# Expert numbers packed five to a word and loaded once into TensorE's registers

## What is computed

```
gates = softmax(xt @ Wg.T)                  # 16 experts
scores, inds = top_k(gates, 2)              # two experts for each token
scores = scores / sum(scores)
h = silu(xt @ We_gate[e].T) * (xt @ We_up[e].T)
y_sel = h @ We_down[e].T                    # for the two experts e of the token
y = sum(y_sel * scores) + sigmoid(xt @ Wsg.T) * shared_expert(xt)
```

## Time and profile before

| | us |
|---|---|
| median of 3 runs without the profiler | 518.58 |
| lowest and highest of them | 518.02, 519.61 |
| span of the profiled execution | 535.7 |
| TensorE busy in it | 516.2 (96%) |
| VectorE busy | 401.4 (75%) |
| ScalarE busy | 277.7 (52%) |
| GpSimd busy | 173.2 (32%) |

### The profile page before, as it was taken

One profiled execution on the slowest core, in us unless ns is written; L12 is line 12 of the kernel. 1 busy time (PEld: TensorE's weight loads), 2 busy tenths in 40 slices (PEclk: granted clock), 3 DMA queues, 4 the chain that ended last, 5 costly groups with the idle time before them and its releaser, 6 DMA issues.

```text
span 535.7 us, 10052 instructions
## 1 busy us (share of the span) xinstructions
PE 516.2 (96%) x3475; PEld 470.2 (88%) x3475; DVE 401.4 (75%) x842; ACT 277.7 (52%) x466; POOL 173.2 (32%) x161
## 2 busy tenths in 40 slices
PE   8999999999999699998999999999999999999997
PEld 6898898898888689988889989898989898989897
DVE  6997466898985466666666458998796969697986
ACT  4696865246652354444444545654453627272751
POOL 0001121101027565566662170517060424224302
PEclk9999999999999899999999999999999999999999
DMA  8926275122025355774456550443034111212112
GB/s 308 411 111 256 90 284 216 32 59 60 31 79 165 121 159 158 226 246 159 162 157 146 167 179 12 113 163 89 20 111 166 59 60 50 61 39 81 39 40 80
DMA packets 29840, 69.16 MB, mean 129 GB/s; under 512 B 4992, under 2 KB 9472, under 8 KB 28768
## 3 DMA queue, kind: packets, MB, share of 16 engines
q1 hardware_dynamic: 22496, 49.68, 25.8%
q0 software_dynamic: 6864, 18.75, 13.1%
q10 hardware_dynamic: 432, 0.09, 0.1%
HBM read 41.24 MB, written 27.26 MB: 128 GB/s over the span
## 4 chain that ended last, share of the span: by engine, by line
PE 81%; DVE 8%; issue 3%; another core or an unknown queue 3%; ACT 2%; DMA 1%; POOL 0%; SPq 0%; POOLq 0%; DVEq 0%; ACTq 0%
PE ps L771 52%; PE ps L981 9%; PE ps L777 6%; PE ps L911 6%; PE ps L1013 4%; PE ps L866 1%; ACT blk_xT L1105 1%; DVE blk_xT L1311 1%; PE ps L928 1%; DVE pT L1311 1%; DMA rows_y<-ytab,slot 1%; DVE probs_f L1646 1%; PE ps L875 1%; DVE place_hot L1497 1%
## 5 line engine op out<-in xcount | busy, mean ns | idle before, releaser
L758 POOL DMA_INDIRECT rows_y<-ytab,slot x64 | 77.6, 1213 | 148.1 <-DVE acc L1661 131.7
L738 POOL DMA_INDIRECT blk_x<-rows,row x79 | 81.0, 1025 | 79.4 <-DVE row L1512 30.5
L771 PE MATMUL ps<-vv,pT 128*128 128x258 f32 x768 | 97.6, 284 | 0.0
L771 PEld LDWEIGHTS ps<-vv,pT 128*128 128x128 f32 x768 | 95.2, 189 | 1.0
L771 PE MATMUL ps<-xT,shared_w 128*128 128x512 f32 x384 | 92.7, 394 | 0.4 <-DVE sil L1389 0.3
L771 PEld LDWEIGHTS ps<-xT,shared_w 128*128 128x128 f32 x384 | 70.7, 188 | 15.5 <-issue 0.9
L771 PE MATMUL ps<-qT,xbT_hi 128*128 128x512 f32 x256 | 79.3, 391 | 0.0
L981 PE MATMUL ps<-expert_w,blk_xT 128*128 x474 | 66.9, 290 | 5.8 <-DVE blk_xT L1311 5.3
L981 PEld LDWEIGHTS ps<-expert_w,blk_xT 128*128 128x128 f32 x474 | 59.5, 191 | 8.4 <-issue 8.3
L771 PEld LDWEIGHTS ps<-qT,xbT_hi 128*128 128x128 f32 x256 | 47.0, 188 | 9.2
L1299 ACT ACTIVATE probs_f<-probs_f 128x1024 f32<-128x1024 f32 x32 | 33.5, 1048 | 35.4 <-DVE probs_f L1646 35.4
(11 more groups left out here) (166 smaller groups left out, 857.7 us busy)
## 6 DMA issues: line engine op xcount, KB each, us to landing
ytab<-blk_y SPq DMA_DIRECT2D x40, 256.0 KB
keys<-xT SPq DMA_DIRECT2D x8, 1024.0 KB, 6.1
stage_e<-in_experts SPq DMA_DIRECT2D x16, 384.0 KB, 3.1
rows<-xn SPq DMA_DIRECT2D x8, 512.0 KB, 3.5
xbT_hi<-keys SPq DMA_DIRECT2D x8, 512.0 KB
xbT_lo<-keys SPq DMA_DIRECT2D x8, 512.0 KB
out<-acc SPq DMA_DIRECT2D x32, 128.0 KB
acc<-in_x SPq DMA_DIRECT2D x7, 512.0 KB, 9.0
```

Of the source, the lines that this page charges most:

```text
L738: e.indirect_dma_start(out=blk_x[:, q, n, :], out_offset=None, in_=rows, in_offset=bass.IndirectOffsetOnAxis(ap=row[:, 2 * b + n:2 * b + n ...
L758: e.indirect_dma_start(out=rows_y[:, r, k, :], out_offset=None, in_=ytab, in_offset=bass.IndirectOffsetOnAxis(ap=slot[:, k, i:i + 1], axis=0),
L771: ins = e.matmul(dst, stationary(p, k), moving(q, k), start=(n == 0), stop=(n == total - 1))
```

## The change

Expert numbers are below 16, so they fit in 4 bits (`BITS`). VectorE first clamps the 80 numbers in float (`blk_m`), and then packs five (`PACK`) into one by Horner's rule, sofar * 16 + next, four times, on 16 numbers at once. The last of the four writes integers to `blk_e`, now 16 words. TensorE loads all 16 words with one TENSOR_LOAD at the place of the first one of before; the other 19 are gone. `expert_of[n]` becomes an expression, shift right and mask, which is worked out in the registers at each block's gate and up products, once for a block (the lowest of five needs no shift). The down products go on from a register that the gate and up products left. The count that TensorE waits for in `routed` grows from 21 to 25.

```diff
+BITS = 4
+PACK = 5
...
         if 0 < b < PAIRS:
-            if b % 2 == 0:
-                steps.append(("blk_ids", b))
             steps.append(("blk_gate_up", b))
...
-        ROUTED = {"ek": 2, "gap": 3, "hot": 6, "totals": 7, "summed": 14, "slots": 18, "blocks": 21}
+        ROUTED = {"ek": 2, "gap": 3, "hot": 6, "totals": 7, "summed": 14, "slots": 18, "blocks": 20 + PACK}
...
-                    _, values = nc.values_load_multi_w_load_instructions(
-                        blk_e[0:1, 2 * b:2 * b + 4], engines=[mybir.EngineType.PE], min_val=0, max_val=NE - 1,
+                    _, packed = nc.values_load_multi_w_load_instructions(
+                        blk_e[0:1, :], engines=[mybir.EngineType.PE], min_val=0, max_val=(1 << BITS * PACK) - 1,
...
-                    for n, value in enumerate(values):
-                        expert_of[2 * b + n] = value
+                    for n in range(USED):
+                        expert_of[n] = (packed[n // PACK] >> (BITS * (n % PACK))) & (NE - 1)
...
-                        e.tensor_scalar(blk_e[:, :], blk_f[:, :], float(NE - 1), None, ALU.min).then_inc(routed, 1)
+                        e.tensor_scalar(blk_m[:, :, :], blk_f[:, :].rearrange("p (r j) -> p r j", j=PACK), float(NE - 1),
+                                        None, ALU.min).then_inc(routed, 1)
+                        for j in range(PACK - 2, -1, -1):
+                            e.wait_ge(routed, at + PACK + 1 - j)
+                            sofar = blk_m[:, :, PACK - 1] if j == PACK - 2 else blk_s[:, j + 1, :]
+                            e.scalar_tensor_tensor(out=blk_e[:, :] if j == 0 else blk_s[:, j, :], in0=sofar,
+                                                   scalar=float(1 << BITS), in1=blk_m[:, :, j], op0=ALU.mult,
+                                                   op1=ALU.add).then_inc(routed, 1)
```

More of the change, by code:

```diff
@@ L488, in build @@
         blk_f = own("blk_f", [P, BLOCKS])
-        blk_e = own("blk_e", [P, BLOCKS], I32)
+        blk_m = own("blk_m", [P, BLOCKS // PACK, PACK])
+        blk_s = own("blk_s", [P, PACK, BLOCKS // PACK])
+        blk_e = own("blk_e", [P, BLOCKS // PACK], I32)
         bqk = own("bqk", [P, 2, KD])
```

## The result

The changed kernel takes 518.93 us (median of 20 runs, 518.26 to 520.10), the kernel before 518.0 us (20 runs beside them, 517.2 to 519.61). The ratio is 1.0016, with a 95% interval from 1.001 to 1.0022: slower by 0.5 to 1.1 us. That lies within the 0.3% that were called no change, but on the other side of the forecast of 518.2: 0.4 us less was forecast, 0.9 us more came. (The prediction had 518.58 us for the kernel before, the median of three runs; twenty give 518.0.)

What follows compares the result with a forecast made beforehand. TensorE was taken to bound the kernel. 518.58 - 1.0 (late completions) + 0.6 (longer load) + 0 (register instructions) + 0 (VectorE) = 518.2 us, range 515.5 to 520.3.

Steps and rivals of the forecast that it cites:

- the first term: Among the blocks: TensorE's completions told late behind loads would go with the nineteen loads, -1.0 us.
- the load of pair 24 holds completions back: Late blocks: waits behind this load read as completions told late, 0.94 us lost in two pairs.
- the 17 us between span and median: Profiled execution of the kernel before, 17.1 us over its median: most waits among the blocks taken as absent without the profiler.
- The 3 us: Stretch of the blocks: about 20 us not TensorE's work less 17.1, the most late completions could cost in the median.
- The sign that I named against it: Last load, at 293.1 us with gathers over: ScalarE waits only 0.28 us, so loads may not delay completions.
- The long load: The one remaining load, ahead of the first blocks, brings 16 words instead of four: a stall of +0.6 us.
- Rival D: Long load alone at the first load's price per word, no gain: 520.0 us, by the skill's page 521.1; chance 0.06.
- The register instructions: On TensorE's sequencer at each block: 142 added, about 0.1 us each, hidden by its lead, 0 us.
- Rival C: Sequencer bounds each pair's gate and up start, bare register instructions behind the wait: 520.6 us for eight pairs; chance 0.06.
- VectorE: Packing ahead of the blocks: four chained instructions, 0.84 us, absorbed by idle time, 0 us.
- The profiled span: Profiled execution after the change: near 528 us if loads hold completions back, 536 if not.

Runs made afterwards that it cites:

- e5: The changed kernel itself beside the kernel before, on a chip where the kernel before takes about 538.5 us: 538.62 us, ratio 1.0005.
- e9: Kernel before with block tokens brought from fixed rows by SyncE's plain transfers instead of GpSimd's gathers: 527.86 us, kernel before beside it 540.19.
- e1: Changed kernel with the sixteen packed words loaded a second time right behind the first load, odd blocks using the second copy: 538.58 us, ratio 1.0002.
- e15: Changed kernel with the sixteen words loaded twice, fixed rows by SyncE and the first keys' transfers issued by ScalarE: 527.6 us.
- e18: Changed kernel with its load behind the last wide products, fixed rows by SyncE, keys' transfers spread over pairs 13, 18, 23 and 28: 524.72 us.
- e17: Kernel before with fixed rows by SyncE and the first keys' four transfers issued by ScalarE at pairs 13, 18, 23 and 28: 524.69 us.
- e4: Kernel before, all twenty loads kept, with 158 register instructions added (numbers times 16, shift and mask per block): 541.19 us, ratio 1.0044.
- e7: Kernel before with 158 register instructions added and all loads kept, run again on a second chip: 541.72 us, ratio 1.0057.
- e12: Kernel before with 158 register instructions added, all loads kept, and fixed rows by SyncE instead of gathers: 531.97 us.
- e14: Changed kernel with fixed rows by SyncE and the first keys' transfers issued by ScalarE: 525.75 us.
- e16: Changed kernel with its load behind the last wide products, fixed rows by SyncE and the first keys' transfers issued by ScalarE: 526.15 us.

## Why the prediction was wrong, and where it was right

**The step that failed is the first term**, -1.0 us for late completions behind the loads. It came from two readings. One was that the load of pair 24 holds completions back, by the earlier trace rows. e5 has such waits, the same rhythm of two pairs and the same span without a load among the blocks; e9 has all the loads and none of the waits. What the runs show in place of the -1.0 is 0. The other was that the 17 us between span and median are the profiler's. They go with the chip: the runs of the kernel before gave 538.5 us there. This reading happened to keep the term small, since it left 3 us to gain; but it was a wrong reason, and that was luck. The 3 us weren't there either. They came from taking all forty pairs at 2.80 us, and in the changed kernel's trace three pairs take 3.52, 3.52 and 3.70 because products of other steps stand in them, 2.3 us of work. The sign that I named against it, no wait behind the last load, was the right one to follow: at 293.1 us there is still a load, and the gathers are over.

**The long load**, +0.6 us, was right in mechanism and about right in size: 1297 ns for 16 words, 81 ns a word against my 83, so 1.30 us against 1.33, and 0.72 us of stall. The price was per word, near enough; a second load of sixteen right behind the first took 1.12 us in e1 and 1.11 in e15. The Trainium skill ("Runtime: NRT & Kernel Launch", section "Instruction fetch mechanics") gives about 200 ns a register, by which I had estimated 3.2 us for the sixteen; for this load from SBUF the trace disagrees, with 1.30. Rival D, which had this end, fell.

**The register instructions**, 0, were right in the steady pace: pairs stay at 2.80 us, and e18 against e17 shows no loss. One is 36 ns long and holds the sequencer for about 0.1 us (two cost 0.19), as I had taken it. But the term is not quite 0: I had priced the two that stand bare wherever TensorE waits for VectorE's copy at 0.1 to 0.25 us, and left them out because few such waits would be left. One is left at pair 2 in the changed kernel's trace, and the two cost 0.19 us there. Rival C had the right mechanism for another kernel: where the loads stay, as in e4, e7 and e12, the instructions come with 2.6 to 4.1 us. It did not come about because the change takes the loads away at the same time.

**VectorE**, 0: right as far as the trace shows; the four operations took about 0.85 us, 147.84 to 148.69, as worked out, and the last `row_f` sum wasn't later than the execution as a whole.

**The sum** with the first term at 0, the load at 0.72 and one bare pair of register instructions at 0.19 is 518.0 + 0.9 = 518.9, against 518.93 measured. The two places are read from traces; that they are the loss is supported and not proved by a run on its own: doubling the load costs more (e15 over e14, 1.9 us, a part of it the clock), and with the load covered no loss is seen (e18, to within 0.8 us). One rival stands: the wait of 1.25 us at 227.00 us, for a store, if it is in most runs of the changed kernel and in few of the kernel before. The changed kernel with the load moved was never timed with its gathers on a chip of the 518 kind; on those of the 538 kind it made no difference. A version that beats both kernels wasn't found: with everything hidden the change can only come back to the time before.

**The profiled span**, 528 or 536, was neither: 518.0, a span of the other kind of chip, where the changed kernel's runs have 516.3 to 518.1.

## What to carry to other kernels

Compare two profiles only after their spans have been held against medians of the same chip; here a span 17 us over its own median meant that the trace was of other conditions, not that the profiler took a toll. Before a wait is put down to an instruction that stands next to it in time, look for a place where the one occurs without the other, as in the earlier trace rows. A step on TensorE's sequencer was free here up to the array's queued work, so one long step cost what many short ones didn't: look where the widest products stand and put it behind them. In the traces that closed the gap; that it saves the time was not measured. And count all that stands in one lead: loads and register instructions were each hidden alone, and not together.

## What the runs showed of the hardware

- The same kernel took 518.0 and 518.37 us on two occasions and 538.5 to 540.2 us on four others, each of these on another chip. On the slow ones the engines wait among the gathers for completions that the rows can't attribute, and late in the blocks the array loses 0.5 us a pair (3.27 to 3.33 against 2.80). With plain transfers instead of the gathers the late pairs take 2.80 us on such chips too (e9).
- TENSOR_LOAD into TensorE's sequencer took 81 to 83 ns a word from SBUF (four in 0.33 us, sixteen in 1.29 to 1.30 us; a second load of sixteen right behind, 1.11 us). Single loads of four took longer, 0.46 to 1.15 us, three to eight of the twenty in each of seven traces, with and without the gathers.
- Six narrow products in the array's queue cover 0.73 us of the sequencer's work. Behind the wide ones a load of 1.29 us left no gap. A load of 0.33 us with two register instructions behind it left the array idle where it started 0.33 us or less ahead of the four turns (e12), and not where it started 0.8 us ahead.
- Register instructions (ALU_OP) are 36 ns long; two of them, bare behind a wait, cost 0.19 us.
- In two traces the long load's stall right behind a wait of 1.7 to 1.8 us for rows came with the lower clock, 0.54 and 0.66 on average in the next 7.5 and 5 us; in e15 18 products took 4.18 us in place of 2.38. With a wait of 1.2 to 1.7 us and no stall behind it the clock stayed full (e9, e12, e16).
